# Eight indirect stores of a batch: at one place, or at eight consecutive places

## What is computed

```python
x = layernorm(x + attention(x))        # 16 heads of 16, rotary, ALiBi bias
shared = silu(X @ sW1 + sb1) @ sW2 + sb2
logits = X @ routing_W.T + expert_bias
activation = sqrt(softplus(logits))
top_vals, top_idx = top_k(activation, 2)       # 2 of 8 experts for each token
routed = sum over the two of top_vals * (silu(X @ rW1[e] + rb1[e]) @ rW2[e] + rb2[e])
x = layernorm(x + shared + routed)
```

## Time and profile before

| | us |
|---|---|
| median of 3 runs | 1753.69 |
| lowest and highest | 1753.49, 1765.55 |
| the profiled execution, its own time | 1758.38 |
| its span, first to last instruction | 1756.6 |
| mean granted TensorE clock | 0.916 of full |

### The profile page before, as it was taken

How to read it: one execution, slowest core, us unless ns; L and a number is a source line. 1 busy time by engine, 2 the same in 40 slices (tenths; PEclk the granted TensorE clock), 3 DMA queues, 4 the chain that set the end, 5 groups by cost and what they waited for, 6 DMA issues and landing times.

```text
span 1756.6 us, 33407 instructions
## 1 busy us (share of the span) xinstructions
PE 1494.1 (85%) x11096; PEld 812.6 (46%) x11096; DVE 1161.4 (66%) x2641; ACT 1031.6 (59%) x1766; POOL 723.8 (41%) x662
## 2 busy tenths in 40 slices
PE   3887989898898999999889998888999897977764
PEld 1433434444454454544445554444444454545643
DVE  5775767676877575666776776758767665533356
ACT  0265656565566576766656675656656675753633
POOL 0233354544435434343545535363354533232444
PEclk7699999899899999999999999999998998977887
DMA  5335243333343444444454545445454555436853
GB/s 181 100 118 160 81 123 101 105 115 111 96 135 122 138 137 148 134 143 140 134 167 155 163 138 165 149 144 164 141 152 148 177 163 178 122 117 190 272 187 118
DMA packets 189924, 251.74 MB, mean 143 GB/s; under 512 B 67837, under 2 KB 104794, under 8 KB 189754
## 3 DMA queue, kind: packets, MB, share of 16 engines
q1 hardware_dynamic: 177514, 216.96, 40.4%
q0 software_dynamic: 11520, 31.47, 5.6%
q10 hardware_dynamic: 720, 1.16, 0.2%
HBM read 157.78 MB, written 95.90 MB: 144 GB/s over the span
## 4 chain that ended last, share of the span: by engine, by line
PE 54%; DVE 14%; SPq 11%; DMA 8%; issue 7%; another core or an unknown queue 3%; ACT 2%; POOL 1%; ACTq 0%; DVEq 0%; POOLq 0%
PE pS L605 15%; PE pV L648 10%; DVE negm L893 6%; PE pG L670 5%; PE pG L781 3%; PE pG L679 3%; PE pS L611 3%; DMA rb<-d_rec 2%; DMA d_rec<-scr 2%; PE pG L773 2%; PE pG L692 2%; SPq L410 2%; PE pG L754 2%; SPq L454 2%
## 5 line engine op out<-in xcount | busy, mean ns | idle before, releaser
L893 DVE TENSOR_REDUCE negm<-pS 128x1 f32<-128x512 f32 x1024 | 660.2, 683 | 351.7 <-PE pS L611 296.8
L1294 ACT ACTIVATE ee<-pT,slp 128x512 f32<-128x512 f32 x1024 | 651.0, 684 | 271.3 <-PE pT L632 212.9
L605 PE MATMUL pS<-ka,qa 62*128 62x512 f32 x1024 | 491.8, 512 | 162.1 <-DVE negm L893 103.9
L626 PE MATMUL pT<-qa,ka 64*128 64x512 f32 x1024 | 489.9, 511 | 12.4 <-ACT ee L1294 11.4
L605 PEld LDWEIGHTS pS<-ka,qa 62*128 62x128 f32 x1024 | 199.9, 195 | 409.8 <-issue 361.9
L648 PE MATMUL pV<-ee,vv 128*32 128x512 f32 (+1 forms) x2048 | 295.9, 652 | 1.5 <-issue 1.2
L611 PE MATMUL pS<-mAB,tri 64*128 64x64 bf16 x2048 | 244.7, 201 | 0.0
L632 PE MATMUL pT<-mAB,tri 64*128 64x64 bf16 x2048 | 241.8, 199 | 0.0
L1450 POOL TENSOR_TENSOR raw<-raw,rope 128x512 f32<-128x512 f32 x60 | 76.8, 1280 | 366.5 <-DVE sh L923 366.5
L626 PEld LDWEIGHTS pT<-qa,ka 64*128 64x128 f32 x1024 | 198.0, 193 | 25.7 <-issue 13.2
L611 PEld LDWEIGHTS pS<-mAB,tri 64*128 64x128 bf16 x2048 | 120.5, 100 | 137.5 <-issue 99.2
(11 more groups left out here) (175 smaller groups left out, 2128.1 us busy)
## 6 DMA issues: line engine op xcount, KB each, us to landing
d_part<-parts SPq DMA_DIRECT2D x64, 512.0 KB
qa<-d_part SPq DMA_DIRECT2D x384, 64.0 KB
wb<-in_wb SPq DMA_DIRECT2D x88, 256.5 KB
xg<-d_x SPq DMA_DIRECT2D x88, 256.0 KB
d_y<-yb SPq DMA_DIRECT2D x88, 256.0 KB
ka<-d_part SPq DMA_DIRECT2D x128, 128.0 KB
xT<-in_xT SPq DMA_DIRECT2D x16, 512.0 KB
ka<-d_part SPq DMA_DIRECT2D x128, 64.0 KB
```

What stands on the lines that cost most here:

```text
L605: e.matmul(pS[:, k, :], qa[g % 4][r, i, t * 128:t * 128 + 128].bitcast(F32R), ka[g % 4][r, i, :].bitcast(F32R), start=True, stop=False)
L626: e.matmul(pT[:, k, :], ka[g % 4][r, i, kt * 128:kt * 128 + 128].bitcast(F32R), qa[g % 4][r, i, :].bitcast(F32R), start=True, stop=False)
L893: e.tensor_reduce(negm[:, g % 2, j, t + k:t + k + 1], pS[:, k, :], AX, ALU.max, negate=True).then_inc(s_max, 1)
L1294: e.activation(ee[:, w % 2, k, j, :], pT[:, k, :], ACT.Exp, scale=slp[:, 6, h:h + 1]).then_inc(s_exp, 1)
```

## The change

The eight stores of a batch stand at offsets 78 to 85, one at each, in the same order; only the first has the waits, as before.

```diff
-SCATTER = (81, 81)
+SCATTER = (78, 79, 80, 81, 82, 83, 84, 85)
...
-        def scatter(b, n):
+        def scatter(b, k):
 
             g = GROUP_OF[b]
-            if n == 0:
+            n, t = divmod(k, 4)
+            if k == 0:
                 e.wait_ge(s_x1, b + 1)
                 e.wait_ge(s_pos, b + 1)
                 if g > 1 and b == LAST_OF[g - 1] + 1:
                     for i in range(3):
                         e.wait_ge(xg_in[i], 16 * ((FIRST_BLOCK[g - 1] + 2 - i) // 3))
-            for t in range(4):
-                e.indirect_dma_start(d_x[g % 2], bass.IndirectOffsetOnAxis(pos[:, b % 2, n, t:t + 1], 0),
-                                     x1[b % 2][:, t, :], None).then_inc(rows_w, 16)
+            e.indirect_dma_start(d_x[g % 2], bass.IndirectOffsetOnAxis(pos[:, b % 2, n, t:t + 1], 0),
+                                 x1[b % 2][:, t, :], None).then_inc(rows_w, 16)
...
-            for n in range(2):
-                if 0 <= (b := due(s, SCATTER[n])) < SPARSE:
-                    scatter(b, n)
+            for k in range(8):
+                if 0 <= (b := due(s, SCATTER[k])) < SPARSE:
+                    scatter(b, k)
```

## The result

The changed kernel takes 1710.11 us (median of 4 runs, 1698.76 to 1713.23) against 1754.63 for the kernel before measured beside it (4 runs, 1753.49 to 1765.55): ratio 0.972, 95% interval [0.966, 0.978]. The profiled execution took 1709.87 us, against 1758.38 before. The forecast was 1723 with a range of 1705 to 1756: the direction and what stalls the kernel hold, the gain was 44.5 us instead of 31.

The account below looks back on a forecast made before the run. TensorE coming late behind runs of indirect stores was taken as the bound: 37.1 + 16.2 = 53.3 us, less 18.9 and 3.6, left 31. 1753.69 - 31 = 1722.7, say 1723; range 1705 to 1756, the forecast's own 1708 to 1737.

Parts of the forecast that it names:

- What bounds it, and the stall: TensorE's results come late behind each batch's run of eight indirect stores; stalls worth 37.1 us over nine batches.
- signs named beforehand: Remote waits under a quarter, unknown pieces under 1%, clock above 0.916, more line 917 waits, none at line 1112.
- The give-back by the reciprocals: Sums' way through DRAM: part of the gain returns as waits for reciprocals, 2.1 us a batch, 18.9 in all.
- nine batches of the sum: Batches 0, 1, 2, 4, 5, 6, 8, 9 and 10, over which the gain was counted.
- Batches 3, 7 and 11: VectorE builds the table while most of the burst passes under it; no gain counted.
- Batches 12 to 14: Stores meet gathers in 12 and 13, and nothing stands between them in 14; no gain counted.
- The clock: TensorE's granted clock is 0.50 after it has stood; 1.8 us a batch, 16.2 us over nine.
- The run of three: Three stores in a row on GpSimd cost 0.4 us a batch, 3.6 us over nine.
- `base`: VectorE needs the eighth store 12.5 us after the shuffle; it lands at 11.5, 1 us to spare, cost 0.
- rival (c): Eighth store, with a landing of 6.25 us, comes too late for `base`; VectorE and TensorE stop; 1772 us, chance 0.10.
- ScalarE's copy: The copy for block 1 waits for rotate instructions, 0.5 us late; cost 0, at worst 6 us.
- Rival (a): Something else at place 17 holds TensorE, so moving stores changes nothing; 1754 us, give or take 5, chance 0.17.

Follow-up runs that it names:

- experiment 3: Changed kernel with the stores at offsets 78, 79, 80, 81, 83, 84, 85, 86, giving four pairs; 1720.36 us on chip B, ratio 0.975 to the kernel before.
- Experiment 2: Changed kernel with the eight stores two places later, at offsets 80 to 87; 1744.02 us on chip B, ratio 0.989 to the kernel before.
- Experiment 1: Changed kernel with all eight stores in one run at offset 78; 1784.31 us on chip B, ratio 1.011 to the kernel before.

## Why the prediction was right, and where its terms were off

- **What bounds it, and the stall (right).** Most of the signs named beforehand came: runs 2, 3, 2, 1; VectorE's remote waits at 10.7 of 41.3 us (just over the quarter that I named, and ScalarE's at 12.9 of 40.7, further over it); the clock up to 0.929; line 1112 without a wait. The chain's unknown share is 1% rounded; its four pieces of over 1 us sum to 13.6 us, 0.8%. They lie at runs of four and more gathers, which the change does not touch. "Remote" is a lower bound of the stall: in batch 9 of the kernel before the same gap stands in the list as waits for line 611 (3.79 us, ending at 1059.17), and the waits under that name fell too, from 296.8 to 278.8 us.
- **The give-back by the reciprocals (the step that failed).** The prediction took 18.3 us per eight places as the floor that the sums' way sets, and 2.1 us a batch, 18.9 in all, as given back to it. In the changed kernel the second eight places of batch 1 took 325.35 - 308.93 = 16.4 us, and on C 15.6. The 18.3 is a floor, but of its own eight places only: line 917 waits 1.29 us for `rb` at their end, before and after alike (the rows below), and has no wait at the end of the eight places ahead of them. I had carried it over from an interval to its neighbour. The sixteen places of batch 1 became 7.9 us shorter (46.3 to 38.4), which is the 7.9 that the prediction had worked out and then cut to 5.8. The waits of line 917 went from 64.8 to 64.0 us in all, not up by 18.9. Without this term the sum was 53.3 - 3.6 = 49.7 us, against 48.5 between the two profiled executions (1758.38 and 1709.87). That this is so close is in part luck, as the batches show.

Line 917 on VectorE in the kernel before, at the end of the second and of the third eight places of batch 1:

```profile
336.44 0.68 DVE L917 TENSOR_TENSOR pvs<-pvs,rb 128x512 f32<-128x512 f32 x1
...
355.87 0.69 DVE L917 TENSOR_TENSOR pvs<-pvs,rb 128x512 f32<-128x512 f32 x1 [1.29 <-DMA rb<-d_rec]
```

and in the changed kernel:

```profile
326.12 0.68 DVE L917 TENSOR_TENSOR pvs<-pvs,rb 128x512 f32<-128x512 f32 x1
...
345.48 0.69 DVE L917 TENSOR_TENSOR pvs<-pvs,rb 128x512 f32<-128x512 f32 x1 [1.29 <-DMA rb<-d_rec]
```

- **The same by batches.** By the starts of line 1303, four intervals a batch: batch 0 gains 2.3 us (81.0 to 78.7; 3.0 are given back in its last interval), batch 1 7.2 (82.9 to 75.8), batch 2 3.9 (81.5 to 77.6). All nine batches of the sum gain 41.9 us, 4.7 each, where the prediction had 31 / 9 = 3.4 with the give-back and 49.7 / 9 = 5.5 without. So some is given back, but later than I put it (3.0 us in batch 0 two intervals later) and less than half of it. Batches 3, 7 and 11, counted as nothing, lose 1.8 together. Each batch is one sample of each kernel.
- **Batches 12 to 14 (too low).** I counted no gain there. The line 1303 starts lose 1.2 us in batch 12 and gain 5.3 in batch 13 and 2.4 in the one interval of batch 14, 6.5 in all. With 0.9 us ahead of batch 0's first start and 1.0 behind the last one the sum is 41.9 - 1.8 + 6.5 + 0.9 + 1.0 = 48.5, the gain of the span but for rounding. So what the nine batches fall short of 49.7 is made up by terms that the prediction put at nothing.
- **The clock (right in direction, its size bounded only).** The time at half speed fell by 52 us; work done in it takes twice as long, so this is worth at most 26 us, against 16.2 in the sum. With 30.6 us off VectorE's remote waits the two make up to 57 us, of which 48.5 arrived.
- **The run of three (small, as assumed).** No remote wait lies beside one, and experiment 3, which has none, is not measurably faster; the sum had 3.6 us.
- **`base` (right, and close).** From the end of the shuffle to line 1112 it is 12.6 us in the changed kernel's batch 1 (predicted 12.5), with no wait, and store 7 starts 8.8 us after that shuffle (320.52 against 311.71), as predicted. Experiment 2 shows how near the edge is: two places more and 13 of the waits are there. The landing, 2.6 us, is the 2.7 that was assumed, and not rival (c)'s 6.25.
- **A bound that its own terms don't give.** The low end of the forecast's own range, 1708, is said to be all 53.3 us less half of the give-back; that is 53.3 - 9.5 = 43.8 and 1710. Nothing hangs on it.
- **ScalarE's copy (right).** Its wait for `parts` went from 2.4 to 5.2 us in all; nothing of that shows.
- **Rival (a).** The traces say no: on B the stall went to place 14 with the stores, on A it went away when they were spread. The Trainium skill's page "SBUF — State Buffer", section "Who interferes with whom", states that TensorE and ScalarE never wait on anyone and that a DMA never contends with a compute engine. On C the trace agrees (no remote wait beside a run of eight); on A it does not (VectorE waits up to 5.5 us for TensorE's results beside such a run), and there the measurement decides. The time by that rule was 1754 us, and 1710 came on A; on C the kernel behaves nearly as it says.

On C, what is the remaining 0.4%? VectorE's line 1105 is one candidate. Kernel before, then changed kernel, both on C, by line:

```profile
L1105 DVE SCALAR_TENSOR_TENSOR hs<-th,zb 128x512 f32<-128x512 f32 x16 | 20.5, 1282 | 0.0
```

```profile
L1105 DVE SCALAR_TENSOR_TENSOR hs<-th,zb 128x512 f32<-128x512 f32 x16 | 11.9, 744 | 0.0
```

After the burst it began at 316.41 us beside a GpSimd rotate instruction (316.12, 1.29 us) and took 2.78 us; with the stores spread it stands elsewhere and takes 0.86. That is 8.6 us in all, about the 7 that were measured, and it fits what the same section of the page says, that a VectorE instruction with two inputs in SBUF contends with a GpSimd one that reads SBUF. No run moved this line alone, so it is a reading, not shown. On A the same line went from 17.0 to 14.5 us only.

## What to carry to other kernels

A wait for "remote" in a program on one core is worth following: set it beside the order of GpSimd's DMAs. Where TensorE's results come late behind a run of four or more indirect DMAs, break the run with work that GpSimd has anyway; runs of two or three were short enough, two runs of four stores nearly so, and the last store must still be in before its reader. Measure such a change on more than one chip: here it was worth 2.8% on one and 0.4% on another. And a floor read from one interval holds for that interval: before it is carried to the next, look whether the wait that makes it one stands there too.

## What the hardware showed that I had not expected

- **The stall is there on one chip and not on another.** The same kernel with the same burst takes 1754 us on A, 1764 on B and 1699 on C. VectorE's remote waits are 41.3 us on A and absent on C; the mean clock is 0.916 and 0.930. The kernel's DMA traffic is the same (251.74 MB, 189,924 packets in both traces). Experiment 1 shows on B that a run of eight stalls TensorE there too. What differs between the chips is not known, nor whether it is the chip itself or a state that it was in: there are two or three chips here, and all 61 runs of the kernel before on C, in two lots, are faster than any on A or B.
- **The stall looks like a late report, then a stop.** In batch 1 on A the matmuls are in the record on time, VectorE is released by them 3.5 us later, and then TensorE itself is short of work; the longest such wait of VectorE is 5.5 us. Whether the write of the semaphore or the end of the matmul is late, the trace can't tell, since the ends of matmuls are modelled.
- **An indirect store's own time on GpSimd hardly depends on its neighbours:** 982 ns as the mean in the burst, 1031 when spread.
